# Other places in the loop order of an attention kernel: PV tiles, rows of maxima, stacks and the input load

## The reference

```python
scores = jnp.einsum('bhqd,bhkd->bhqk', q, k) * SCALE
scores = jnp.where(causal[None, None, :, :], scores, -jnp.inf)
probs = jax.nn.softmax(scores, axis=-1)
y = jnp.einsum('bhqk,bhkd->bhqd', probs, v)
...
x = x + jnp.tanh(g_xattn[0]) * _L0_xattn_ref(_layernorm(x, axis=-1), ctx_1024, ...)
x = x + jnp.tanh(g_ffn[0]) * _L0_ffn_ref(_layernorm(x, axis=-1), ...)
```

## Time and profile before

| | |
|---|---|
| median of 3 runs | 1872.76 us (1872.36 to 1877.73) |
| the profiled execution | 1872.91 us, span from first to last instruction 1871.2 us |
| mean granted TensorE clock | 0.974 of full |
| TensorE matmul busy | 1745.9 us, 93% of the span |
| VectorE, ScalarE, GpSimd busy | 1075.4, 932.2, 931.7 us |
| attention part | up to about 812 us, the experts behind it |
| a steady round of the attention | about 45.3 us, rounds 3 to 14 |

### The profile page before, as it was taken

How to read it: one execution, slowest core, us unless ns; L and a number is a source line. 1 busy time by engine, 2 the same in 40 slices (tenths; PEclk the granted TensorE clock), 3 DMA queues, 4 the chain that set the end, 5 groups by cost and what they waited for, 6 DMA issues and landing times.

```text
span 1871.2 us, 40632 instructions
## 1 busy us (share of the span) xinstructions
PE 1745.9 (93%) x12838; PEld 1026.6 (55%) x12902; DVE 1075.4 (57%) x3480; ACT 932.2 (50%) x1812; POOL 931.7 (50%) x1026
## 2 busy tenths in 40 slices
PE   4899999999999999818999999999899999999997
PEld 1455555555555555413656565656556565656565
DVE  3788888888888888466443434343343434343421
ACT  2467777777777776523343434343343434343332
POOL 6377788777778885551332324242323232424222
PEclk8899999999999999959999999999999999999999
DMA  6767777778777786365654545656636455555221
GB/s 168 161 172 197 191 199 194 197 197 200 199 196 193 199 199 151 86 162 147 129 103 85 104 85 105 130 78 124 106 67 112 94 96 105 86 96 82 46 32 23
DMA packets 408333, 247.85 MB, mean 132 GB/s; under 512 B 289303, under 2 KB 389759, under 8 KB 408191
## 3 DMA queue, kind: packets, MB, share of 16 engines
q1 hardware_dynamic: 383183, 212.39, 49.4%
q0 software_dynamic: 24576, 33.57, 11.2%
q10 hardware_dynamic: 432, 0.13, 0.0%
HBM read 118.63 MB, written 58.72 MB: 95 GB/s over the span
## 4 chain that ended last, share of the span: by engine, by line
PE 51%; DVE 3%; issue 1%; DMA 1%; ACT 0%; POOL 0%; POOLq 0%; DVEq 0%
PE bank L1108 11%; PE bank L1107 11%; PE bank L1109 11%; PE bank L1125 6%; PE bank L1123 6%; PE bank L1124 6%; DVE h L1225 0%; DVE top_at L1175 0%; DVE h L1228 0%; ACT h L1153 0%; DVE work L1178 0%; DVE top L1173 0%; DMA rows<-tokens,row_now 0%; DMA out<-y,row_now 0%; DMA tokT<-rows 0%
## 5 line engine op out<-in xcount | busy, mean ns | idle before, releaser
L1073 POOL DMA_INDIRECT out<-y,row_now x128 | 202.0, 1578 | 605.9 <-ACT y L1160 581.3
L687 DVE CUSTOM_DVE_ANT_0 masked<-bank,causal 128x128 bf16<-128x128 f32 (+3 forms) x1024 | 449.6, 485 | 62.1 <-PE bank L459 60.0
L571 ACT ACTIVATE prob<-bank 128x512 f32<-128x512 f32 x640 | 360.1, 595 | 140.4 <-PE bank L479 103.1
L1225 DVE TENSOR_TENSOR h<-bank,silu 128x512 f32<-128x512 f32 x256 | 176.4, 689 | 392.5 <-PE bank L1109 258.6
L1153 ACT ACTIVATE h<-h 128x512 bf16<-128x512 f32 x256 | 161.2, 630 | 346.2 <-DVE h L1225 324.5
L1228 DVE TENSOR_TENSOR h<-h 128x512 bf16<-128x512 f32 x256 | 177.4, 693 | 179.4 <-ACT h L1153 171.8
L1125 PE MATMUL bank<-downT,h 128*128 128x256 bf16 x1024 | 279.1, 273 | 0.0
L1124 PE MATMUL bank<-downT,h 128*128 128x256 bf16 x1024 | 279.1, 273 | 0.0
L1123 PE MATMUL bank<-downT,h 128*128 128x256 bf16 x1024 | 279.1, 273 | 0.0
L459 PE MATMUL bank<-ks,qs 96*128 96x128 bf16 (+3 forms) x1024 | 254.9, 306 | 19.2 <-DMA ks<-k_parts 10.2
L1108 PE MATMUL bank<-tokT,gateT 128*128 128x512 bf16 x511 | 194.7, 381 | 35.4 <-DMA tokT<-rows 28.9
(11 more groups left out here) (141 smaller groups left out, 2675.4 us busy)
## 6 DMA issues: line engine op xcount, KB each, us to landing
q_parts<-q_sb SPq DMA_DIRECT2D x64, 192.0 KB, 4.5
k_parts<-k_sb SPq DMA_DIRECT2D x64, 192.0 KB, 3.8
qs<-q_parts SPq DMA_DIRECT2D x64, 192.0 KB, 3.5
ks<-k_parts SPq DMA_DIRECT2D x64, 192.0 KB, 3.1
x_t<-in_x SPq DMA_DIRECT2D x16, 512.0 KB, 4.2
ctx_t<-in_ctx SPq DMA_DIRECT2D x16, 512.0 KB, 5.5
qs<-q_parts SPq DMA_DIRECT2D x64, 128.0 KB, 3.3
ks<-k_parts SPq DMA_DIRECT2D x64, 128.0 KB, 3.0
```

Of the source, the lines that this page charges most:

```text
L571: nc.scalar.activation(prob[:, gr % 2, h0:h0 + nh, POFF[tiles[0]]:POFF[tiles[0]] + w], sc_bank[SC_BANK[k]][:, 0:nh * w].rearrange("p (h w) ...
L687: last = nc.vector.tensor_tensor_reduce(masked[:, (gr * NMAX + k) % 2, part], max_bank[max_at(gr, k)][:, part], causal[:, T - w:T], 1.0, L ...
L1073: nc.gpsimd.indirect_dma_start(out_rows, bass.IndirectOffsetOnAxis(ap=row_now[:, par, c, s:s + 1], axis=0), y[:, c % 2, s, :], None, compu ...
```

## The change

`extra` gets other places for many pieces; nothing else is changed, and no piece is added or removed. The core of the diff:

```diff
         0: {0: [("mrow", b - 1, 3)],
-            1: [("ln1+", b + 1, 0), ("yt+", b - 1, 0), ("pv", b - 1, 1, 0), ("yt", b - 1, 0)],
-            2: [("xsplit", b + 1, 0)],
-            3: [("mt", b - 1, 3), ("ln1+", b + 1, 1), ("xturn", b + 1), ("xsplit", b + 1, 1), ("pv", b - 1, 1, 1), ("pv", b - 1, 1, 2)],
-            4: [("csplit", b + 1, 0), ("o", b - 2, 0, 0), ("o", b - 2, 0, 1), ("mt+", b - 1, 3)],
+            1: [("pv", b - 1, 1, 0), ("ln1+", b + 1, 0), ("yt", b - 1, 0)],
+            2: [("xsplit", b + 1, 0), ("yt+", b - 1, 0), ("ln1+", b + 1, 1)],
+            3: [("pv", b - 1, 1, 1), ("pv", b - 1, 1, 2), ("mt", b - 1, 3), ("xturn", b + 1), ("xsplit", b + 1, 1)],
+            4: [("mt+", b - 1, 3), ("o", b - 2, 0, 0)],
+            5: [("csplit", b + 1, 0), ("kstack", b, 2)],
+            6: [("o", b - 2, 0, 1), ("o+", b - 2, 0), ("o", b - 2, 1, 0)],
...
-        1: {0: [("qstack", b, 2), ("kstack", b, 2)],
-            1: [("yturn", b - 1, 0), ("yt+", b - 1, 1), ("mrow", b, 0), ("ysplit", b - 1, 0)],
-            2: [("mt", b, 0), ("mt+", b, 0), ("ln2", b - 2, 0)],
-            3: [("ln2", b - 2, 1), ("pv", b - 1, 2, 0), ("q", b + 1, 0, 0)],
+            8: [("cturn", b + 1)],
+            10: [("yt", b - 1, 1), ("qstack", b, 2)]},
+        1: {0: [("ysplit", b - 1, 0), ("yt+", b - 1, 1)],
+            1: [("ln2", b - 2, 0), ("pv", b - 1, 2, 0)],
+            2: [("mt+", b, 0), ("ln2", b - 2, 1), ("mt", b, 0)],
+            3: [("mrow", b, 0), ("q", b + 1, 0, 0), ("yturn", b - 1, 0)],
...
-            6: [("q", b + 1, 1, 1), ("kstack", b, 3), ("q+", b + 1, 1)],
-            8: [("k", b + 1, 0, 0), ("ln2+", b - 2, 1), ("pv", b - 1, 2, 2)],
-            9: [("xs", b - 2), ("ln2+", b - 2, 0), ("pv", b - 1, 2, 3)]},
+            7: [("k", b + 1, 0, 0)],
+            8: [("ln2+", b - 2, 1)],
+            9: [("ln2+", b - 2, 0), ("pv", b - 1, 2, 2), ("kstack", b, 3)],
+            10: [("pv", b - 1, 2, 3), ("qstack", b, 3)]},
...
-            3: [("load", b + 2), ("pv", b - 1, 3, 0)],
-            5: [("qstack", b, 3), ("yt", b - 1, 2), ("yt+", b - 1, 2), ("pv", b - 1, 3, 1)],
-            7: [("pv", b - 1, 3, 2), ("qstore", b + 1), ("vaug", b)],
-            8: [("pv+", b - 1, 3), ("mrow", b, 1), ("pv", b - 1, 3, 3), ("xt", b - 2, 0), ("xt+", b - 2, 0)],
+            2: [("qstore", b + 1)],
+            3: [("mt", b, 1), ("pv", b - 1, 3, 0), ("mt+", b, 1)],
+            6: [("pv", b - 1, 3, 1), ("pv", b - 1, 3, 2), ("vaug", b)],
+            8: [("pv", b - 1, 3, 3), ("pv+", b - 1, 3), ("ysplit", b - 1, 1), ("xt+", b - 2, 0), ("xt", b - 2, 0)],
+            9: [("load", b + 2)],
...
-        3: {0: [("kstore", b + 1)],
-            3: [("ll+", b - 2), ("pv", b, 0, 0), ("ll", b - 2), ("v", b + 1, 0, 0), ("kstack", b + 1, 0)],
+        3: {0: [("mrow", b, 1), ("res", b - 1)],
+            1: [("mt+", b, 2), ("yt+", b - 1, 3), ("kstore", b + 1), ("yt", b - 1, 3), ("mt", b, 2), ("pv", b, 0, 0)],
+            3: [("ln1", b + 2, 0), ("ll", b - 2), ("v", b + 1, 0, 0), ("kstack", b + 1, 0), ("ll+", b - 2)],
```

More of the change, by code:

```diff
@@ L106, in steps @@
-        2: {1: [("pv+", b - 1, 2), ("k+", b + 1, 0), ("k", b + 1, 0, 1)],
-            2: [("mt", b, 1), ("mt+", b, 1)],
-            3: [("load", b + 2), ("pv", b - 1, 3, 0)],
-            4: [("k", b + 1, 1, 0), ("k", b + 1, 1, 1), ("k+", b + 1, 1)],
-            5: [("qstack", b, 3), ("yt", b - 1, 2), ("yt+", b - 1, 2), ("pv", b - 1, 3, 1)],
-            7: [("pv", b - 1, 3, 2), ("qstore", b + 1), ("vaug", b)],
-            8: [("pv+", b - 1, 3), ("mrow", b, 1), ("pv", b - 1, 3, 3), ("xt", b - 2, 0), ("xt+", b - 2, 0)],
-            9: [("res", b - 1), ("xt+", b - 2, 1)],
-            10: [("xt", b - 2, 1)]},
@@ new lines, in steps @@
+            2: [("xsplit", b + 1, 0), ("yt+", b - 1, 0), ("ln1+", b + 1, 1)],
[3 more added lines that the diff above has]
+            6: [("o", b - 2, 0, 1), ("o+", b - 2, 0), ("o", b - 2, 1, 0)],
+            7: [("o+", b - 2, 1), ("csplit", b + 1, 1), ("o", b - 2, 1, 1), ("pv+", b - 1, 1), ("pv", b - 1, 1, 3)],
@@ new lines, in steps @@
+        2: {1: [("k", b + 1, 0, 1), ("pv+", b - 1, 2), ("xs", b - 2), ("k+", b + 1, 0)],
+            2: [("qstore", b + 1)],
+            3: [("mt", b, 1), ("pv", b - 1, 3, 0), ("mt+", b, 1)],
+            4: [("k", b + 1, 1, 0), ("k+", b + 1, 1), ("yt+", b - 1, 2), ("k", b + 1, 1, 1)],
+            5: [("yt", b - 1, 2)],
+            6: [("pv", b - 1, 3, 1), ("pv", b - 1, 3, 2), ("vaug", b)],
+            8: [("pv", b - 1, 3, 3), ("pv+", b - 1, 3), ("ysplit", b - 1, 1), ("xt+", b - 2, 0), ("xt", b - 2, 0)],
+            9: [("load", b + 2)],
+            10: [("xt", b - 2, 1), ("xt+", b - 2, 1)]},
@@ new lines, in steps @@
+        3: {0: [("mrow", b, 1), ("res", b - 1)],
+            1: [("mt+", b, 2), ("yt+", b - 1, 3), ("kstore", b + 1), ("yt", b - 1, 3), ("mt", b, 2), ("pv", b, 0, 0)],
+            2: [("qstack", b + 1, 0)],
+            3: [("ln1", b + 2, 0), ("ll", b - 2), ("v", b + 1, 0, 0), ("kstack", b + 1, 0), ("ll+", b - 2)],
+            4: [("mrow", b, 2), ("v+", b + 1, 0)],
+            5: [("lt+", b - 2), ("v", b + 1, 0, 1), ("yturn", b - 1, 1), ("lt", b - 2)],
+            6: [("pv", b, 0, 1), ("save", b - 2)],
+            7: [("v", b + 1, 1, 0), ("kstack", b + 1, 1)],
+            8: [("v", b + 1, 1, 1)],
+            9: [("v+", b + 1, 1)],
+            10: [("pv+", b, 0), ("qstack", b + 1, 1), ("pv", b, 0, 2), ("pv", b, 0, 3), ("ln1", b + 2, 1)]},
```

16 lines of the change are left out of this document (3 added, 13 removed).

## The result

The changed kernel takes 1889.84 us (median of 6 runs, 1883.53 to 1891.79) against 1873.17 us for the kernel before, measured beside it. The ratio is 1.0075 with a 95% interval of 1.006 to 1.0091: it is slower by three quarters of a percent. (The two medians alone would give 0.9%, the means 0.7%.) The forecast was 1880.5 with a range of 1867 to 1890. The direction is right, the size is half of what came, and the median is inside the range by 0.2 us. The profiled execution of the changed kernel took 1888.40 us, 15.5 more than that of the kernel before (1872.91). The last output product of the attention starts 14.6 us later (808.1 instead of 793.5), so the part behind the barrier holds only 0.9.

The account below looks back on a forecast made before the run. TensorE was taken as the bound in the attention part, everything behind it unchanged. Terms -8.4 - 6.3 + 7.3 + 6.2 + 7.6 + 1.3 gave +7.7 us on 1872.9: 1880.5 us, range 1867 to 1890.

Parts of the forecast that it names:

- A: First group's scores: TensorE's wait for the row of maxima goes, as SyncE sends stacks and row earlier; -8.4 us.
- B: Second group's maxima: gaps waiting for VectorE go, with a PV tile moved in front; -6.3 us.
- C: Start of a round: ScalarE normalizes a second pair of tiles before an exp, so TensorE waits at scores; +7.3 us.
- D: End of second group: key product ahead of the ninth scores unit makes ScalarE late for the third group; +6.2 us.
- E: Second group's row of maxima lands late behind the load on SyncE, 0.85 us in 13 rounds; +7.6 us net.
- rival 1: The second group's row lands in time despite the load, so E costs nothing: 1869.5 us; chance 0.17.
- F: Start of the run: round 1's load, now behind the store of q, delays the first stack of keys; +1.3 us.
- G: PV tiles: one 32-column run fewer by joining, one more by separating from the gate products; 0.21 saved, 0.21 lost: 0.
- rival 2: ScalarE keeps up, so C and D are 0: 1867.0 us; chance 0.11, with rival 1 as well 0.04.
- Rival 3: The moves cancel: gains at A and B return in full at C, D and E: 1873 us; chance 0.10.
- Rival 4: A longer backlog: each load takes 6.5 instead of 5.5 us, 13 us more: 1893 us; chance 0.08.
- the steady round: Sign announced for the attention loop: a steady round of 45.8 to 46.1 us instead of 45.3.

Follow-up runs that it names:

- experiment 9: Kernel before with only the first PV tile of the old batch's group 2 moved to step 1 of the second group: 1875.3 us, ratio 1.0003.
- experiment 4: Changed kernel with the second pair of normalized tiles back at step 3, behind the exp of scores unit 3: 1887.1 us, ratio 1.0074.
- experiment 5: On experiment 1, both halves of the output product at step 4 again: 1860.8 us, ratio 0.9926.
- experiment 8: Kernel before with only group 2's stacks sent earlier and the first group's row of maxima ahead of the transpose: 1867.3 us, ratio 0.9961.
- experiment 6: Changed kernel with the first key product back at step 8 of the second group instead of step 7: 1886.5 us, ratio 1.0064.
- experiment 7: On experiment 1, the first key product back at step 8 of the second group: 1861.7 us, ratio 0.9927.
- experiment 1: Changed kernel with the second group's row of maxima ahead of the 1 MB load on SyncE: 1865.8 us, ratio 0.9956.
- experiment 12: Changed kernel with the edits of experiments 1, 5 and 7, and in round -1 the load ahead of the store of q: 1856.1 us, ratio 0.991.
- experiment 10: Kernel before with only the third PV tile of group 3 joined to the second at step 5: 1873.6 us, ratio 0.9998.
- experiment 3: Changed kernel with the second group's row of maxima ahead of the load in rounds 0 and 1 only: 1878.6 us, ratio 1.0022.
- experiment 11: On experiment 1, the new batch's first PV tile directly ahead of the gate products again: 1861.2 us, ratio 0.9941.

## Why the prediction was right in its direction and short in its size

**A was right**, in size and place: -8.4, no wait at the first group's scores. The row goes out at offset 18.4 instead of the forecast 17.6. Alone it is worth 7 us.

**B was right in size and incomplete in its cause.** The gaps are gone, 6.3 us. But the PV tile alone gives nothing (experiment 9). The step "the first PV tile in front of these maxima, so VectorE is done in time" asked only what VectorE owes the maxima, not what else waits for VectorE when TensorE gets there sooner.

**C was right in size** (0.50 us a round for 0.52) **and put the weight on the wrong one of its two causes.** The prediction spoke of the second pair of tiles ahead of the exp, and named the output product as a condition. Experiments 4 and 5 turn this around: the order on ScalarE only chooses the unit that stalls, the product decides whether one does.

**D was right**: 0.32 us a round at the two scores units and 0.14 at the PV tile of the third group, which the prediction didn't name, together 5.8 for 6.2. Its cause, the key product, is shown by experiments 6 and 7. But its sentence that A's gain is spent at once by D is wrong: A alone (experiment 8) brings nothing back at these units.

**E is the term that was mis-sized**: +7.6 forecast, +12.5 measured. Its mechanism and its steady size were right: issue at offset 29.8 for 29.9, landing at 34.7 for 34.9, TensorE there at 34.0 for 34.05. Behind the load the row takes 4.2 us where a clear queue gives 1.8. The Trainium skill (DMA: Bandwidth & Descriptors, Anatomy of one DMA — SWDGE (gpsimd) path) gives a fixed cost of about 2.0 us for a DMA issued from GpSimd. This row is issued from SyncE; it is near that figure in a clear queue (1.8, in experiment 1 too), and far from it behind the load, so rival 1 fell. The step that was mis-sized is "0.85 us in the 13 rounds with a load": the number of round 8 was taken for all. Of the 4.9 us that it lacks, rounds 0 to 3 give 3.7 (7.1 in sum for 3.4) and rounds 4 to 13 give 1.9 (9.6 for nine times 0.85); 0.8 go off because the kernel before already lost 4.2 us there and not 3.4. The wait comes in 14 rounds, not 13. That the load and the row behind it take longer in five of these rounds is read from the trace; why they do, no run shows.

**What the sum didn't have is the second price of a long wait.** At the two longest of the first waits the clock fell. The kernel before had one such drop in round 0, the changed one has one in round 0 and a longer one in round 1: about 1.9 us more by the rows, and 1.7 more while the pipeline empties. The prediction treated TensorE's clock as unchanged. Together with 0.9 us in the experts this is more than the 2.6 us that the table leaves open, so small gains stand against it elsewhere; these stay unassigned.

**F was too small**: 2.8 us for 1.3, beyond the bound of 2.0 that the prediction gave. Its cause holds in every trace: the first maxima come at 44.2 to 45.1 us in the eight with the load behind the store of q, at 41.5 to 42.5 in the six with it ahead. What an earlier start is worth at the end isn't shown: in experiment 12 round 0 gave it back, by two waits of 1.0 us and a drop of the clock, and one trace can't tell whether that is so in every run.

**G fits as a balance of the changed kernel**: the joining saves 0.2 (read from the kernel before in experiment 10; in the changed kernel it wasn't taken away alone), the separation costs 0.26. What the prediction called "one run more" is worth 3 to 5 us when undone on experiment 1. The Trainium skill (TensorEngine Tiling (Array Packing), Key Properties) says that changing the tiling mode drains TensorE; the 0.11 us between the tile's two durations agree with it. The join alone gives nothing on the kernel before, since the tile was cover (experiment 10).

The rivals: rival 1 fell with E, rival 2 with C and D. Rival 3, that the moves cancel, was wrong for this kernel. But its mechanism is real: experiment 6 shows the gain of one place waiting at the next. Rival 4 came nearest in time (1893), and its reason holds in part: it had each load take 6.5 us instead of 5.5, and the load's second half takes 5.9 to 6.6 us in rounds 0, 1, 2, 6 and 7, but 4.9 to 5.3 in the others. The forecast took round 8 for all rounds, rival 4 the slowest; both happen.

Of the announced signs, those of A, B, C, D and the steady round hold (46.1 us from round 4 to 13, 45.2 before). Of E's waits six of 14 are above the announced 0.5 to 1.3 us. The total wait for `m_sb` is 15.3 instead of 7 to 13, and the first maxima are at 44.8 instead of 43.2.

## What to carry to other kernels

In an in-order DMA queue, send the small transfer that somebody waits for ahead of the big one that nobody needs yet: one swap of neighbours was worth 22 to 24 us here, more than the rest of the change together. Price a wait round by round and not by one steady round, and don't take the clock as given: a wait of about 2 us can take it along, and did in some traces here and not in others. And before crediting a move, ask what the same engine meets next: three of the moves here (one of PV, the join, the key product under a fixed wait) removed their stall exactly, and met it again within ten microseconds.

## What the runs showed of the hardware

A wait of 1.6 and one of 2.4 us of TensorE in the first two rounds came with its lower clock for about 3 and 7 us; with the waits taken away the clock stayed up (22 against 39 operations between 76 and 80 us), and round 2 started 8.5 us earlier for 4.0 us of waits.

The length of the wait doesn't settle it. Among these traces the clock fell at waits of 1.8 us (round 2 of experiment 10), 2.2 (round 7 of experiment 4) and 2.4 (start of round 4 of experiment 12), and stayed up at waits of 1.8 (round 2 of the kernel before), 1.9 (round 3 of experiment 3), and 2.3 (round 3 of experiment 6, start of round 4 of experiment 7).

Two transfers of 4 KB took 4.2 us directly behind 1 MB in the same queue in a steady round, up to 5.5 us in others, and 1.8 us ahead of it.

The changed kernel's runs spread over 8 us (1883.5 to 1891.8) and the kernel before's over 6 (1872.4 to 1878.4). The longer runs are those with the lower mean clock: the changed kernel's two short runs (1883.5 and 1884.2) have 0.974 of full, the four others (1888.4 to 1891.8) 0.971 to 0.973. Of the kernel before's 23 runs on the chip of experiments 3, 10, 11 and 12, the seven under 1872 us have 0.975 or 0.976, the eleven above 1874 us have 0.972 to 0.974. So part of the spread is the clock; whether that is cause or consequence of other waits isn't shown.
